# VectorE empties the attention's value and score banks, in a newly interleaved order of work

## The reference, cut to what matters

```python
loc  = pw(dw(gelu(patch_embed(x))))                      # layer L
g    = gelu(pw(dw(gelu(conv1x1(wavelet_packet(x))))))    # layer G
h    = (1 - gate) * loc + gate * conv1x1(g)              # W2 and "mix"
h    = relu(pw(dw(h)));  h = relu(pw(dw(h)))             # layers F1, F2
tok  = layernorm(tokens(pw(dw(loc + h))))                # layer F3, 1 + 196 tokens, then 128 of text
xh   = layernorm(concat(tok, txt))                       # T = 325 tokens
q, k, v = mlp(xh), mlp(xh), mlp(xh)                      # two linear layers each, gelu between
y    = (mask * (q @ k.T) / sqrt(192 * 64)) @ v           # mask: a band of 64 keys, no softmax
h2   = tok_and_text + layernorm(y)
out  = h2 + bitlinear(gate(bitlinear(h2)))               # feed-forward with rounded weights and activations
```

## Time and profile before

| | |
|---|---|
| median of 3 runs | 1259.73 us (1259.23 to 1260.78) |
| the profiled execution | 1260.41 us, its span 1258.5 us |
| PE busy | 1139.4 us (91%) |
| DVE busy | 1007.7 us (80%) |
| ACT busy | 1001.6 us (80%) |
| POOL busy | 895.9 us (71%) |

### The profile page before, as it was taken

How to read it: one execution, slowest core, us unless ns; L and a number is a source line. 1 busy time by engine, 2 the same in 40 slices (tenths; PEclk the granted TensorE clock), 3 DMA queues, 4 the chain that set the end, 5 groups by cost and what they waited for, 6 DMA issues and landing times.

```text
span 1258.5 us, 19622 instructions
## 1 busy us (share of the span) xinstructions
PE 1139.4 (91%) x5674; PEld 857.1 (68%) x5674; DVE 1007.7 (80%) x2868; ACT 1001.6 (80%) x2581; POOL 895.9 (71%) x924
## 2 busy tenths in 40 slices
PE   3577999999999999999999999999999997979544
PEld 2455787778777878787777778777878785656222
DVE  0666678898989899898989898989999897855643
ACT  2364777898999898989899899989898988776543
POOL 2345477888878787878887888878887877765421
PEclk8797999999999999999999999999999998989655
DMA  8110101010101010101000010101010000000000
GB/s 311 39 44 1 46 1 46 2 56 6 57 6 54 7 52 11 49 14 47 15 26 34 6 57 6 57 6 53 8 49 14 10 15 9 16 8 11 11 8 13
DMA packets 21514, 40.26 MB, mean 32 GB/s; under 512 B 2656, under 2 KB 18208, under 8 KB 19104
## 3 DMA queue, kind: packets, MB, share of 16 engines
q1 hardware_dynamic: 21408, 39.01, 9.0%
HBM read 31.02 MB, written 7.99 MB: 31 GB/s over the span
## 4 chain that ended last, share of the span: by engine, by line
PE 83%; DVE 6%; ACT 5%; issue 2%; DMA 2%; POOL 2%; SPq 1%; DVEq 0%; POOLq 0%; ACTq 0%
PE bank L388 14%; PE bank L490 7%; PE bank L408 7%; PE bank L409 7%; PE bank L366 4%; PE bank L367 4%; PE bank L411 3%; PE bank L413 3%; PE bank L412 3%; PE bank L502 3%; PE bank L511 3%; PE bank L432 2%; PE bank L433 2%; PE bank L369 2%; DVE bank L1219 2%; PE bank L370 2%
## 5 line engine op out<-in xcount | busy, mean ns | idle before, releaser
L1219 DVE SCALAR_TENSOR_TENSOR bank<-padA,c_col,bank 128x406 f32<-128x406 f32 x560 | 358.5, 640 | 9.7
L388 PE MATMUL bank<-x_sb,w_emb 128*128 128x392 f32 x576 | 215.3, 507 | 21.2 <-ACT padB L727 19.9
L803 ACT ACTIVATE prod<-padB,c_col 128x196 f32<-128x196 f32 x432 | 178.1, 458 | 8.9 <-DVE padB L1240 5.1
L1672 POOL TENSOR_TENSOR yg<-y_f,c_gout 128x512 f32<-128x512 f32 (+1 forms) x96 | 122.1, 1272 | 58.8 <-DVE y_f L1409 46.4
L388 PEld LDWEIGHTS bank<-x_sb,w_emb 128*128 128x128 f32 x576 | 105.4, 196 | 77.2 <-ACT padB L727 21.8
L803 ACT ACTIVATE early<-padB,c_col 128x196 f32<-128x196 f32 x288 | 125.1, 459 | 6.1 <-POOL accB L1703 6.0
L490 PE MATMUL bank<-w_in,xq 128*128 128x512 bf16 (+1 forms) x384 | 109.1, 410 | 7.7 <-ACT xq L866 7.7
L1390 DVE SCALAR_TENSOR_TENSOR ya<-th,bank 128x512 f32<-128x512 f32 (+1 forms) x96 | 65.3, 680 | 62.6 <-ACT th L872 62.4
L1209 DVE TENSOR_SCALAR bank<-padA,c_col 128x406 f32<-128x406 f32 x80 | 51.1, 639 | 56.4 <-ACT padA L734 48.8
L872 ACT ACTIVATE th<-bank,sm 128x512 f32<-128x512 f32 (+1 forms) x96 | 66.0, 688 | 25.8 <-PE bank L490 25.5
L502 PEld LDWEIGHTS bank<-c_id,r 128*128 128x128 f32 (+1 forms) x384 | 42.2, 148 | 62.6 <-ACT r L852 46.0
(11 more groups left out here) (226 smaller groups left out, 3535.8 us busy)
## 6 DMA issues: line engine op xcount, KB each, us to landing
x_sb<-xt SPq DMA_DIRECT2D x16, 1176.0 KB, 5.4
out<-o_sb SPq DMA_DIRECT2D x64, 96.0 KB
w_sq<-squares SPq DMA_DIRECT2D x1, 3840.0 KB, 15.7
h_sb<-txt SPq DMA_DIRECT2D x32, 51.8 KB
out<-o_sb SPq DMA_DIRECT2D x32, 51.8 KB
h_sb<-txt SPq DMA_DIRECT2D x32, 44.2 KB
w_in<-win SPq DMA_DIRECT2D x1, 1024.0 KB, 17.7
c_row<-broads SPq DMA_DIRECT2D x1, 672.0 KB, 19.3
```

Of the source, the lines that this page charges most:

```text
L388: done = mm(pE[:, 0:2 * N_PATCH], w_emb[:, k, m, :], x_sb[:, k, :], start=k == 0, stop=k == KC - 1)
L803: made = go(grid(prod[ACC[s] ^ 1][:, k, :]), tap_view(padB[min(s, 2)], SIDE, k), ACT.Copy, scale=tapcol(s, 1, k))
L1219: v.scalar_tensor_tensor(grid(acc if k == TAPS - 1 else run), tap_view(pad, ROWS_A, k), tapcol(s, 0, k), grid(run), ALU.mult, ALU.add).the ...
L1672: g.tensor_tensor(yg[0:m, :], y_f[0:m, :], c_gout[0:m, :], ALU.mult).then_inc(f_yg, 1)
```

## The change

The evacuation of values and scores moves to VectorE, with the bias and the mask in the same instruction:

```diff
-            def values_out(a, t):                      # ACT
-                took(a, U_V2 + t)
-                go(v_sb[0:m, t, :, :], src, ACT.Copy).then_inc(at_act, 1)
...
+            def values_out(a, t):                      # DVE
+                dve.wait_ge(at_full, a * UNITS + U_V2 + t + 1)
...
+                v.tensor_tensor(v_sb[0:m, t, :, :], src, wide(row("vb2", m), 2), ALU.add).then_inc(v_ready, 1)
-            def scores_out(a, img):                    # ACT
-                go(sc0[:, img, 0:SEAM], src[:, 0:SEAM], ACT.Copy)
-                go(sc1[:, img, :], src[:, SEAM:SEAM + n1], ACT.Copy)
-                go(sc2[0:n2, img, :], src[0:n2, SEAM + n1:SEAM + n1 + n2], ACT.Copy).then_inc(at_act, 1)
+            def scores_out(a, img):                    # DVE
+                dve.wait_ge(at_full, a * UNITS + U_SC + img + 1)
+                v.tensor_tensor(sc0[:, img, 0:SEAM], src[:, 0:SEAM], c_mask[:, 0:SEAM], ALU.mult)
+                v.tensor_tensor(sc1[:, img, :], src[:, SEAM:SEAM + n1], c_mask[:, 0:n1], ALU.mult)
+                v.tensor_tensor(sc2[0:n2, img, :], src[0:n2, SEAM + n1:SEAM + n1 + n2], c_mask[0:n2, 0:n2],
+                                ALU.mult).then_inc(sc_masked, 1)
-            def masked(c, i):                          # POOL
-            def biased_values(c):                      # POOL
```

PE's `took` and `unit_free` now wait for `v_ready` and `sc_masked` where the bank was emptied by DVE. Besides this all five lists are written out anew. The first stage is numbered 0, and PE's copies of the stages are one higher, because block BB of the next pair is now multiplied late in the turn:

```diff
 def turn(it, par, on):                                 # PE
-                if on[5]:
-                    embed_chunk(it - 5, EMB_BB, range(0, 2))
+                if on[0]:
+                    embed_chunk(it, EMB_BB, range(0, 2))      # now late in the list, before layer_F2
 def turn(it, par, on):                                 # ACT
-                if on[0]:
-                    if first(it):
-                        weight_sums()                  # ahead of everything of pair 0
+                if on[0]:
+                    if first(it):
+                        weight_sums()                  # behind products(it, G_, range(8, 9)) of pair 0
```

More of the change, by code:

```diff
@@ new lines, in turn @@
+                if on[1]:
+                    loc_out(it - 1)
+                if on[3]:
+                    mlp_out(it - 3, U_K2, k2, "kb2", ACT.Identity, 1)
+                if on[4]:
+                    rounded_tokens(it - 4, 0)
+                if on[0]:
+                    embed_out(it, EMB_BB)
+                    products(it, G_, range(0, 1))
+                if on[1]:
+                    products(it - 1, F1_, range(0, 1))
+                if on[4]:
+                    gate_tanh(it - 4, 0, par)
@@ new lines, in turn @@
+                if on[0]:
+                    embed_out(it, EMB_GA)
+                if on[4]:
+                    round_tokens(it - 4, par, 5)
+                if on[0]:
+                    products(it, G_, range(6, 7))
+                if on[4]:
+                    gate_tanh(it - 4, 2, par)
+                if on[0]:
+                    products(it, G_, range(7, 8))
+                if on[3]:
+                    mixed_values_out(it - 3, 1)
+                if on[4]:
+                    round_hidden(it - 4, 1)
@@ L1097, in turn @@
+                if on[0]:
+                    products(it, G_, range(8, 9))
+                if on[3]:
+                    mixed_values_out(it - 3, 2)
                 if on[0]:
@@ new lines, in turn @@
+                if on[1]:
+                    f1_out(it - 1)
+                if on[0]:
+                    products(it, L_, range(0, 1))
+                if on[4]:
+                    rounded_tokens(it - 4, 3)
+                if on[1]:
+                    products(it - 1, F2_, range(0, 1))
+                if on[0]:
+                    embed_out(it, EMB_LA)
+                    products(it, L_, range(1, 2))
+                    products(it, L_, range(2, 3))
+                if on[2]:
+                    mlp_out(it - 2, U_Q1, hq, "qb1", ACT.Gelu, 0)
@@ new lines, in turn @@
+                if on[0]:
+                    products(it, L_, range(6, 7))
+                    products(it, L_, range(7, 8))
+                if on[4]:
+                    rounded_hidden(it - 4, 3)
+                if on[0]:
+                    products(it, L_, range(8, 9))
+                if on[4]:
+                    mean_square(it - 4, 4, par)
+                if on[2]:
+                    mlp_out(it - 2, U_V1, hv, "vb1", ACT.Gelu, 1)
+                if on[0]:
+                    mix_out(it)
@@ new lines, in turn @@
+                if on[0]:
+                    taps(it, L_, 2)
+                if on[4]:
+                    hidden_round(4, it - 4, 3, par)
+                if on[0]:
+                    taps(it, L_, 3)
+                    taps(it, L_, 4)
+                if on[4]:
+                    gated(it - 4, 4)
+                    lifted(it - 4, 4)
+                if on[0]:
+                    taps(it, L_, 5)
+                if on[3]:
+                    hidden_bn(it - 3, odd, range(0, 3))
+                if on[0]:
+                    taps(it, L_, 6)
```

1220 lines of the change are left out of this document (571 added, 649 removed).

## The result

The changed kernel takes 1228.82 us (median of 4 runs, 1227.0 to 1230.05) against 1260.26 in the same comparison: ratio 0.9742, 95% interval 0.9729 to 0.9755, 31.4 us less. The profiled execution has a span of 1225.1 us, 33.4 less than before. The first `xT` copy of each pair (ACT) marks the same point of every pair, so the two traces can be laid side by side by it. (The rows of 131.57 before and of 109.25 after are the second and third copy of pair 0; the first starts at 129.92 and 107.61.)

What follows compares the result with a forecast made beforehand. PE, busy for all 67.60 us of a full turn, was taken as the bound. From 1260.4, fill -21, full turns +5, last turns +1 and drain -3 gave 1242.4, predicted as 1242 us, range 1230 to 1257.

Steps and rivals of the forecast that it cites:

- term (a): Fill, pair 0: without the weight sums ahead of BB's evacuation on ACT, the first tap comes 12 to 14 us earlier.
- layer L no longer running beside `ternary_weights`: Fill, pair 0: reason given for the rest of mix's move from 66.92 to 48 to 50 us.
- (b): Fill, turn 1: BB evacuation ahead of the F1 products on ACT; pair 1's first tap 20 to 22 us earlier.
- (c): Fill, turn 2: token norm's wait for POOL has only products behind it; first xT copy near 110 instead of 131.57.
- The first `xT` copy ... should come near 110. So the fill gives 21 us: Fill: xT copy near 110 instead of 131.57; gain 21 us, the mean of 17 to 24.
- with its later start ... 13.0 to 13.1: Full turns, F3 to hidden transposes: DVE needs 13.0 to 13.1 us against PE's 12.8, so PE waits 0.2 to 0.3.
- one turn lacks a BB block on PE ... but DVE keeps its 64.7: +1 us: Pair 15's embedding stretch: PE loses 4.0 us of work, DVE stays at 64.7; +1 us, between 0 and 4.
- Drain: End: POOL's mask and bias leave the way from scores to mixed_values; -3 us, between -6 and +2.
- DVE as the bound: Full turns: DVE keeps its 6.1 us of waits, turns of 70.8 us, +38, some 1275 us; chance 0.12.
- the partial gain: Fill: only the wait behind the weight sums goes, -12, turns cost +6; 1251 us; chance 0.15.
- The third rival: No stall in full turns, and a drain that gives 6 us; 1233 us; chance 0.10.
- The clock rival: Full turns: waits at lifted drop PE's clock to 0.95, turns of 71.2 us, +43, 1285 us; chance 0.03.

Runs made afterwards that it cites:

- The one-edit runs: Weight sums behind pair 0's G products in the kernel before: 1244.8 us; weight sums back ahead of pair 0's BB evacuation in the changed kernel: 1245.12 us.
- the run with BB late: Changed kernel with block BB's evacuation and three G products behind the token norm on ACT, for the fill's first pairs only: 1231.86 us.
- the run with the sums put back: Changed kernel with the weight sums back ahead of pair 0's first embedding evacuation on ACT: 1245.12 us.
- the evacuation alone: Kernel before in its own order, DVE emptying value and score banks with bias and mask, ACT's copies and POOL's two steps gone: 1266.2 us.
- with one step moved: Kernel before in its order with evacuation on DVE, the second value evacuation put behind the other pair's mix: 1261.44 us.
- the run with the old evacuation: Changed kernel's order, but ACT copies values and scores out and POOL adds the bias and masks: 1319.54 us.

## Why the prediction was right and wrong

- *Start, term (a).* Right, and nearly so in size: 12 to 14 us at the first tap were forecast, 15.1 came, of which 1 is an earlier start of PE (14.57 against 15.52). The one-edit runs put the weight sums at 16.2 and 16.3 us. Part of it is the clock: the second embedding block at 4.22 instead of 6.25 us.
- *The rest of the fill.* The marks were right within 1 us, the reasons not, so the hit is in part luck. For `mix` of pair 0 the forecast gave as the reason "layer L no longer running beside `ternary_weights`". That step failed: in both kernels this rounding starts directly behind L's taps (52.99 and 38.19), and in the changed one two of POOL's sums still run beside it, in 1.46 and 1.39 us where those of that size in layer G take 0.60. What shortens the way from the first tap to `mix` from 26.1 to 21.7 us is that POOL gets L's last products earlier and that layer L runs at the full clock. Terms (b) and (c) rest on BB's place on ACT, which the run with BB late puts at 0 to 3 us.
- *The fill beyond pair 0.* The step that failed is "The first `xT` copy ... should come near 110. So the fill gives 21 us": the copy came there, but the fill isn't over with it. The next three pairs took 2.8 us less, which had no term. It comes with the order: the run with the sums put back has 185.66 us there, the one of the evacuation alone 189.18. Half of it is idle time of PE: 0.78 us in each of the turns behind pairs 0 and 1 before, 0.00 and 0.11 after.
- *The full turns.* The step that failed is the DVE side of the stretch from F3 to the hidden transposes, "with its later start ... 13.0 to 13.1". PE's side was right: 739.47 to 752.27, 12.80 us. DVE's `lifted` ended at 751.67, 12.2 after F3, so 0.6 us ahead of PE where 0.2 to 0.3 late was forecast. `nm_tok` alone takes 0.85 us less in it, since POOL's instruction ends just as it starts (745.54 and 745.48); with these 0.85 us `lifted` would end at 752.52, 0.25 behind PE, as forecast (DVE began 0.4 us later than reckoned there, and the rest of its work took 0.35 less). The evacuations cost nearly what was reckoned (0.546 for a value, 0.35, 0.35 and 0.22 for a score, 3.47 a turn against 3.2; the forecast took 0.31 for 192 columns, where the mean of one in that row is 0.351), but the turn's busy time of DVE rose by only 1.9. A cost near the forecast 0.4 us a turn was measured in the old order (0.5 in the run of the evacuation alone), but at a place that the forecast didn't name, `mix` ahead of F3. Forecast +5 for twelve turns, measured -1.7 for ten. Why a turn is 0.15 us shorter with the same PE work wasn't settled.
- *Last turns.* The step "one turn lacks a BB block on PE ... but DVE keeps its 64.7: +1 us" failed: the turns before pairs 14 and 15 are 1.4 and 2.3 us shorter. No block of 4.0 us is missing on PE in them (busy 59.52 and 50.80 us before, 59.30 and 49.70 after), and DVE is busy for 61.42 and 47.92 us, not for 64.7. In the run of the evacuation alone they are 66.56 and 61.68 against 66.33 and 62.34, in sum 0.4 less; so 3.3 of the 3.7 come with the order. Which entry does it stays open.
- *Drain.* -3 was forecast and -3.0 read from the two profiles. With the spread given above it is 0.7 to 3.5, so hitting it was luck, and the reason is borne out for a part only: the evacuation alone gave 0.5 there (135.05 against 135.59) and, with one step moved, 1.3 (134.30).
- *The rivals.* DVE as the bound is refuted by the evacuation alone, the partial gain and the gain eaten before the full turns by the 22.3 us at pair 0. The third rival, no stall in the full turns and 1233, came nearest and was right on the turns, but not on the drain, where it had -6. The clock rival's mechanism exists: waits of 3.1 us brought the clock to 0.95 in the slowest turns of the run with the old evacuation, PE's busy time rising from 67.2 to 70.6. The Trainium skill's "TensorE: Matmul & The Clock Gate", section "HAM oscillation — how this bites in real kernels", tells of a matmul loop that falls back to the slower clock behind the wait of every pass, and that trace agrees: 0.50 behind the wait at 805.7, 0.99 from 815 on. The changed kernel has no such wait.

In sum the terms were -18 and came to -33.4 in the profiled executions: the 15 us of difference are 1 at pair 0, 3 behind it, 7 in the full turns and 5 in the last ones. Order and evacuation don't add: the evacuation alone is +5.9 or 0, the order alone, as placed here, +59, both together -31.

## What to carry to other kernels

A step in an in-order list that waits for a late load, a weight preparation say, is to stand behind all that doesn't need it: that was half of the gain. When work moves between engines, the room it has is the room at one place of the list, not the engine's idle share: 1.4 us more on DVE cost 1.0 of a turn in which it idled for 4. Where PE waits for a few microseconds per step in a chain, count its work at the low clock, and fill the wait with matmuls a little shorter than itself, of later work if there is any (8 rows of block BB ahead of layer L here). That pays where nothing else is late: in the drain it gave 10 us, in the turns with the old evacuation 0.7 to 0.9 of 5.5 us each.
